# Attention on one Trainium2 core: score products as 32-row strips, one per head, with maxima and key mask added by accumulating products

## The reference

```python
N_HEAD = 16
qh = _split(q @ wq.T + bq)          # 8 x 16 x 256 x 8
kh = _split(k @ wk.T + bk)          # 8 x 16 x 512 x 8
vh = _split(v @ wv.T + bv)
scores = jnp.einsum('bhqd,bhkd->bhqk', qh, kh) / jnp.sqrt(jnp.float32(d_head))
# layer 2 only, one mask for all batches:
scores = jnp.where(mask == 0, jnp.float32(-1000000000.0), scores)
# layer 2, self-attention inside the feed-forward part: causal mask
# layer 3 only, one mask of keys per batch:
energy = jnp.where(mask == 0, jnp.float32(-1e+20), energy)
attn = jax.nn.softmax(scores, axis=-1)
out = jnp.einsum('bhqk,bhkd->bhqd', attn, vh)
return out.reshape(b, s, 128) @ wo.T + bo
```

## Time and profile before

| | us |
|---|---|
| median of 3 runs | 2374.96 |
| the 3 runs | 2376.47, 2366.19, 2374.96 |
| span of the profiled execution | 2364.8 |
| PE busy in it | 2118.7 (90%) |
| ACT busy | 1289.5 (55%) |
| DVE busy | 1247.3 (53%) |
| POOL busy | 499.4 (21%) |

### The profile page before, as it was taken

How to read it: one execution, slowest core, us unless ns; L and a number is a source line. 1 busy time by engine, 2 the same in 40 slices (tenths; PEclk the granted TensorE clock), 3 DMA queues, 4 the chain that set the end, 5 groups by cost and what they waited for, 6 DMA issues and landing times. The chain is left out here.

```text
span 2364.8 us, 46942 instructions
## 1 busy us (share of the span) xinstructions
PE 2118.7 (90%) x14264; PEld 1391.1 (59%) x14264; DVE 1247.3 (53%) x3806; ACT 1289.5 (55%) x2226; POOL 499.4 (21%) x1107
## 2 busy tenths in 40 slices
PE   2999975699997999979999978887997999989998
PEld 1555543355555889844554545555885555548887
DVE  5667646566662222256666544444564667642343
ACT  0777752377774444346666644444331787864443
POOL 4221210111211222121111111222232222212221
PEclk9999987699998999979999978788997899999999
DMA  3322310622310000052213011110003423300000
GB/s 81 90 80 54 94 29 0 169 71 64 89 40 10 1 0 0 1 143 67 69 45 85 28 41 42 54 54 10 0 0 101 119 72 76 89 1 1 4 4 10
DMA packets 101314, 117.53 MB, mean 50 GB/s; under 512 B 12710, under 2 KB 68412, under 8 KB 101180
## 3 DMA queue, kind: packets, MB, share of 16 engines
q1 hardware_dynamic: 101180, 115.94, 18.5%
HBM read 70.82 MB, written 45.09 MB: 49 GB/s over the span
## 5 line engine op out<-in xcount | busy, mean ns | idle before, releaser
L929 PE MATMUL ps_s<-kst,qz 96*128 96x512 f32 (+2 forms) x1280 | 601.2, 485 | 60.6 <-DMA qz<-q_parts 40.4
L758 ACT ACTIVATE prob<-ps_t 128x512 f32<-128x512 f32 (+1 forms) x896 | 492.3, 581 | 265.7 <-PE ps_t L941 109.9
L941 PE MATMUL ps_t<-qz,kst 128*128 128x512 f32 (+1 forms) x1152 | 464.5, 407 | 0.5 <-ACT prob L758 0.2
L1313 DVE CUSTOM_DVE_ANT_0 junk<-ps_s,mask_q 128x512 bf16<-128x512 f32 x512 | 342.1, 688 | 167.1 <-PE ps_s L929 160.4
L1304 DVE TENSOR_REDUCE mx<-ps_s 128x1 f32<-128x512 f32 x512 | 334.5, 684 | 138.5 <-PE ps_s L929 137.3
L929 PEld LDWEIGHTS ps_s<-kst,qz 96*128 96x128 f32 x1280 | 256.4, 205 | 237.1 <-DVE mx L1313 59.9
L961 PE MATMUL ps_av<-prob,vaug 128*32 128x256 f32 (+1 forms) x4608 | 363.5, 390 | 3.4 <-ACT avs L794 3.1
L1160 PEld LDWEIGHTS ps_s<-w_ffn,prob 128*128 128x128 f32 x2688 | 315.4, 192 | 8.7
L1160 PE MATMUL ps_s<-w_ffn,prob 128*128 128x128 f32 x2688 | 319.2, 276 | 0.0
L798 ACT ACTIVATE qz<-ps_m 32x1024 fp32r<-32x1024 bf16 x160 | 162.7, 1017 | 152.6 <-PE ps_m L971 149.0
L941 PEld LDWEIGHTS ps_t<-qz,kst 128*128 128x128 f32 x1152 | 225.0, 197 | 33.7 <-issue 9.8
(11 more groups left out here) (200 smaller groups left out, 2403.3 us busy)
## 6 DMA issues: line engine op xcount, KB each, us to landing
kst<-k_parts SPq DMA_DIRECT2D x32, 768.0 KB, 6.1
k_parts<-k_hi SPq DMA_DIRECT2D x64, 256.0 KB, 2.9
qz<-q_parts SPq DMA_DIRECT2D x160, 96.0 KB
q_parts<-q_hi SPq DMA_DIRECT2D x80, 128.0 KB, 2.4
ctxT<-in_ctxT SPq DMA_DIRECT2D x32, 256.0 KB, 4.7
k_parts<-k_lo SPq DMA_DIRECT2D x32, 256.0 KB, 2.9
q_parts<-q_lo SPq DMA_DIRECT2D x40, 128.0 KB, 2.4
w_ffn<-in_F_w SPq DMA_DIRECT2D x18, 256.0 KB, 3.9
```

The costliest lines, as they stand in the source:

```text
L758: nc.scalar.activation(dst, src, ACT.Exp, bias=bias).then_inc(sig["exp_done"], 1)
L929: pe.matmul(ps_s[TURN[i]][:, 0:nk], qz[p][0:96, g, j, q * 128:(q + 1) * 128], kst[p][0:96, g, 0:nk], start=True, stop=True).then_inc(sig[" ...
L941: mm = pe.matmul(dst, kst[p][:, g, kt * 128:(kt + 1) * 128], qz[p][:, g, 2 * half:2 * half + 2, q0:], start=True, stop=mask in (None, "keys"))
L1313: dve.tensor_tensor_reduce(junk[:, TURN[i], 0:nk], src, m, 1.0, -3.0e38, ALU.add, ALU.max, mx[:, buf, i:i + 1])\
```

## The change

- **Strips.** Each head of a group gets 32 partitions of its own: 24 rows of parts, and 8 rows that are ones in `kst` and zeros in q's stack, `qst`. The DRAM scratch has 32 rows per head; the 8 rows are filled once, by four DMAs from `q_lo` and `k_lo`, which POOL fills first. The memsets of `qz` and `kst` go, in the setup and at the start of A2 and A3.
- **s** (L952) becomes a row tile of 32 rows x 128 columns with 512 keys. The order of the eight is now heads 0, 1, 2, 3 for the first 128 queries, then for the others (`HEAD_S`).
- **MT** (L1003, L1005) is now one product that copies `qst` of the group into `ps_m` (by `ident_r`) and two bf16 products that add the transposed maxima in the eight rows of each head. ACT copies the sum into `qmx` (128 x 256, before 32 x 1024). POOL no longer negates, DVE's reduction does.
- **T** (L971) of a unit is one head and two key tiles, two products of 256 queries each on the head's strip, into one bank. The heads run in the order 2, 3, 0, 1 (`HEAD_T`), so a unit's s and T lie on different strips.
- **Key mask (A3).** After each s and each T comes a bf16 product with one row on the same strip and into the same bank (L955, L974), which adds the mask's row. POOL prepares one bf16 row per batch (`mrow`); DVE's maximum is the plain one, ACT's exponential has no bias.
- **Full mask (A2)** and **causal mask (AS)** (L977, L981) stay one product on 128 rows, after the two T of the unit. In AS a unit has 256 + 128 columns, four units a group, two at k = 0 and two at k = 3.
- **Splits.** But in AS, ACT reads a projection once (`kf`, `qf`), and POOL makes `k_hi` and `q_hi` from it and then the low part. SP's saves wait for POOL's copy.
- **Loads.** K's and q's stacks are loaded group by group, eight DMAs per batch on a semaphore per group, after both saves; s of a group waits for its own two.
- `prob` is now ordered by head, v (L995) reads it so; its products are the same.

```diff
+HEAD_S = [0, 1, 2, 3, 0, 1, 2, 3]
+HEAD_T = [2, 3, 0, 1, 2, 3, 0, 1]
...
-        qz = [sb(f"qz{p}", [128, NG, HG, S], F32R) for p in range(2)]
+        qst = [sb(f"qst{p}", [128, NG, S], F32R) for p in range(2)]
+        qmx = sb("qmx", [128, 2, S], F32R)
...
-            def load_k(ph, bt):
+            def load_strips(ph, bt):
+
                 p, nk = bt.parity, ATT[ph]["nk"]
                 sp.wait_ge(k_saved[p], saved(ph, bt))
-                rows = scratch["k"][p].rearrange("(g r) w -> r g w", g=NG)[:, :, 0:nk]
-                sp.dma_start(kst[p][0:HG * ROWS, :, 0:nk].bitcast(F32), rows).then_inc(k_stacked[p], 16)
...
                 sp.wait_ge(q_saved[p], saved(ph, bt))
-                for j in range(HG):
-                    rows = scratch["q"][p].rearrange("(g j r) w -> j r g w", g=NG, j=HG)[j]
-                    sp.dma_start(qz[p][ROWS * j:ROWS * (j + 1), :, j, :].bitcast(F32), rows).then_inc(q_stacked[p], 16)
+                for g in range(NG):
+                    sp.dma_start(kst[p][:, g, 0:nk].bitcast(F32), scratch["k"][p][128 * g:128 * (g + 1), 0:nk]).then_inc(stacked[p][g], 16)
+                    sp.dma_start(qst[p][:, g, :].bitcast(F32), scratch["q"][p][128 * g:128 * (g + 1), :]).then_inc(stacked[p][g], 16)
...
+                if ph != "AS":
+                    apart(pool)
+                    pool.tensor_copy(k_hi[:, 0:nk], kf[:, 0:nk]).then_inc(sig["k_hi_done"], 1)
+                pool.wait_ge(sig["k_hi_done"], cnt.at("k_hi_done", ph, bt))
+                pool.tensor_tensor(k_lo[:, 0:nk], kf[:, 0:nk], k_hi[:, 0:nk].bitcast(F32), ALU.subtract).then_inc(sig["k_lo_done"], 1)
...
-                pe.matmul(ps_s[TURN[i]][:, 0:nk], qz[p][0:96, g, j, q * 128:(q + 1) * 128], kst[p][0:96, g, 0:nk],
-                          start=True, stop=True).then_inc(sig["s_ready"], 1)
...
+                mm = pe.matmul(dst, qst[p][strip, g, q * 128:(q + 1) * 128], kst[p][strip, g, 0:nk],
+                               start=True, stop=ATT[ph]["mask"] != "keys")
+                if ATT[ph]["mask"] == "keys":
+                    mm = pe.matmul(dst, ones_b[STRIP * j:STRIP * j + 1, 0:128], mrow[STRIP * j:STRIP * j + 1, p, :], start=False, stop=True)
+                mm.then_inc(sig["s_ready"], 1)
...
-                mm = pe.matmul(dst, kst[p][:, g, kt * 128:(kt + 1) * 128], qz[p][:, g, 2 * half:2 * half + 2, q0:],
-                               start=True, stop=mask in (None, "keys"))
+                bank = ps_t[TURN[turn]]
+                for c in range(2):
+                    kt = 2 * kp + c
+                    dst = bank[:, S * c:S * (c + 1) - seen(ph, kt)]
+                    mm = pe.matmul(dst, kst[p][strip, g, kt * 128:(kt + 1) * 128], qmx[strip, g % 2, seen(ph, kt):],
+                                   start=c == 0 or mask in (None, "keys"), stop=mask is None)
+                    if mask == "keys":
+                        mm = pe.matmul(dst, mrow[STRIP * j:STRIP * j + 1, p, kt * 128:(kt + 1) * 128], ones_b[STRIP * j:STRIP * j + 1, :],
+                                       start=False, stop=True)
...
-                for j in range(HG):
-                    for q in range(QT):
-                        mm = pe.transpose(ps_mb[96:128, S * j + 128 * q:S * j + 128 * (q + 1)],
-                                          mpart[:, g % 2, q, 32 * j:32 * j + 32], ident_b[:, :])
+                pe.matmul(ps_m[:, 0:S], ident_r[:, :], qst[bt.parity][:, g, :], start=True, stop=False)
+                for q in range(QT):
+                    mm = pe.matmul(ps_m[:, 128 * q:128 * (q + 1)], mpart[:, g % 2, q, :], ident_b[:, :], start=False, stop=q == QT - 1)
```

More of the change, by code:

```diff
@@ L41 @@
 HG = 4
-ROWS = 3 * DH
+STRIP = 32
+PARTS = 3
 NG = H // HG
@@ L361, in seen, with pairs, unit, unit_at @@
             return 128 * kt if ph == "AS" else 0
-        def turn_of(ph, g, kt, half):
-            return (2 * (ATT[ph]["nk"] // 128 * g + kt) + half) % 8
+        def pairs(ph):
+            return ATT[ph]["nk"] // (2 * 128)
+        def unit(ph, g, n):
+            return HG * pairs(ph) * g + n
+        def unit_at(ph, k, half):
+            if pairs(ph) == 2:
+                return 2 * k + half
+            return {0: 0, 3: 2}[k] + half if k in (0, 3) else None
+        def chance(ph, g, n):
+            return prob[:, g % 2, HEAD_T[n], :], 2 * (n // HG)
         def slots(ph):
@@ L426, in _ @@
             load_attention("A0", loaded_first)
+            sp.wait_ge(setup_pool, 3)
+            for p in range(2):
+                for n, fill, w in (("q", q_lo, S), ("k", k_lo, SK)):
+                    rest = scratch[n][p].rearrange("(h b c) w -> b h c w", h=H, b=STRIP // DH)[PARTS]
+                    sp.dma_start(rest, fill[:, 0:w].bitcast(F32)).then_inc(strips_filled, 16)
             def load_rest():
@@ L748, in _, with exponentials @@
         def _(act):
-            def exponentials(ph, bt, g, kt, half):
-                p, nkt, q0 = bt.parity, ATT[ph]["nk"] // 128, seen(ph, kt)
-                bias = mcol[:, p, kt:kt + 1] if ATT[ph]["mask"] == "keys" else 0.0
-                wait(act, "st_ready", cnt.at("st_ready", ph, bt, 2 * (nkt * g + kt) + half))
-                if half == 0:
-                    wait(act, "av_ready", cnt.at("av_ready", ph, bt, nkt * g + kt) - 2 * nkt)
-                dst = prob[:, g % 2, kt, 2 * S * half:2 * S * (half + 1)].rearrange("p (j s) -> p j s", j=2)[:, :, q0:]
-                src = ps_t[TURN[turn_of(ph, g, kt, half)]][:, 0:2 * (S - q0)].rearrange("p (j s) -> p j s", j=2)
-                nc.scalar.activation(dst, src, ACT.Exp, bias=bias).then_inc(sig["exp_done"], 1)
+            def exponentials(ph, bt, g, n):
+                nkt = ATT[ph]["nk"] // 128
+                wait(act, "st_ready", cnt.at("st_ready", ph, bt, unit(ph, g, n)))
+                if n % HG == 0:
+                    wait(act, "av_ready", cnt.at("av_ready", ph, bt, nkt * g + 2 * (n // HG) + 1) - 2 * nkt)
+                row, kt = chance(ph, g, n)
+                w = 384 if ph == "AS" else 2 * S
+                nc.scalar.activation(row[:, S * kt:S * kt + w], ps_t[TURN[unit(ph, g, n) % 8]][:, 0:w], ACT.Exp).then_inc(sig["exp_done"], 1)
             def misc(what, ph, bt):
@@ L920, in scores @@
             def scores(ph, bt, g, i):
-                p, nk, j, q = bt.parity, ATT[ph]["nk"], i // 2, i % 2
-                if g == 0 and i == 0:
-                    pe.wait_ge(q_stacked[p], stacked(ph, bt, HG))
-                    pe.wait_ge(k_stacked[p], stacked(ph, bt, 1))
+                p, nk, j, q = bt.parity, ATT[ph]["nk"], HEAD_S[i], i // HG
+                strip = slice(STRIP * j, STRIP * (j + 1))
+                if i == 0:
+                    pe.wait_ge(stacked[p][g], loads_until(ph, bt))
+                    if ATT[ph]["mask"] == "keys" and g == 0:
+                        wait(pe, "mask_conv", cnt.at("mask_conv", ph, bt))
                 if ph == "AS":
@@ new lines, in scores, with scores_T @@
+                mm = pe.matmul(dst, qst[p][strip, g, q * 128:(q + 1) * 128], kst[p][strip, g, 0:nk],
[3 more added lines that the diff above has]
+                mm.then_inc(sig["s_ready"], 1)
+            def scores_T(ph, bt, g, n):
+                p, mask = bt.parity, ATT[ph]["mask"]
+                turn, j, kp = unit(ph, g, n) % 8, HEAD_T[n], n // HG
+                strip = slice(STRIP * j, STRIP * (j + 1))
+                if n == 0:
+                    wait(pe, "mt_read", cnt.at("mt_read", ph, bt, g))
+                wait(pe, "exp_done", cnt.at("exp_done", ph, bt, unit(ph, g, n)) - BACK[turn])
+                bank = ps_t[TURN[turn]]
[7 more added lines that the diff above has]
+                                       start=False, stop=True)
@@ L957, in values @@
                         wait(pe, "v_read", cnt.at("v_read", ph, bt))
[L958 removed]
+                wait(pe, "exp_done", cnt.at("exp_done", ph, bt, unit(ph, g, HG * (kt // 2) + HG - 1)))
                 buf = g % 2
```

153 lines of the change are left out of this document (69 added, 84 removed).

## The result

The changed kernel takes 2468.3 us (median of 4 runs, 2460.68 to 2516.44) against 2372.03 for the kernel before (4 runs), a ratio of 1.038, 95% interval 1.0337 to 1.0423: **slower by 96 us**, where -0.8% was forecast. The ratio leaves out the run of 2516.44, in which the clock was lower than in the other three. The profiled execution spans 2458.5 us, 93.7 more than before.

A forecast was written before the change was run, and what follows sets the result against it. PE sets the pace, DVE is the next wall. A0 and A1 -96, A3 +66, A2 +8, AS +15, starts -13 give -20: span 2345, plus 10 for the median, 2355 us; own range 2315 to 2395, with rivals 2310 to 2545.

The forecast's parts named there:

- Strips side by side: In A0 and A1, s and T on different strips overlap: minus 0.53 us per cycle, 2.12 per group.
- Rivals (1): Strips overlap in columns but their weight loads queue, 0.107 us each: 2448 us, slower; chance 0.14.
- (2): Strips don't overlap at all and a cycle gets 0.045 us longer: 2638 us; chance 0.09.
- Helpers and XT: Per batch, helper products cost 2.0 us in changes of shape; single ACT reads and time around XT give -0.85.
- The 0.2 per change of shape: Wherever tile shape changes between PE products, 0.09 us plus the open weight load is lost, 0.2 us.
- A3: The one-row key mask can't run beside the product it is added to: plus 0.45 us per cycle, +66 us.
- rival (4): A3's masks overlap after all, so A3 gains like A1, -48 instead of +66: 2241 us; chance 0.06.
- A2: The 128-row mask product sits between strips, 0.44 us each; the cycle wins nothing, helpers cost: +8 us.
- AS: Causal mask between short strips and helpers cost, less waiting for K's stack wins: +15 us, range -10 to +60.
- Starts: At stage starts, first scores wait for one group's load, not the whole stack, and A0 loses memsets: -13 us.
- rival (3): Strips use a quarter of the array, so A0 to A3 might fall to AS's granted clock, 0.81: 2546 us; chance 0.13.
- its last sign: The forecast is wrong altogether if A3 is not the stage that loses.

The follow-up runs named there:

- Run 4: Changed kernel with T's heads in the order 0, 1, 2, 3, so a unit's s and T share one strip: 3084.05 us, 1.298.
- run 8: Changed kernel with ACT making k_hi and q_hi in all stages again, POOL only the low parts: 2428.16 us.
- Run 1: Kernel before, with s and T reading only 32 rows of their stacks: 3315.75 us, 1.396 times before.
- runs 2: Kernel before, with five added VectorE reductions in the last group of every batch so that PE waits: 2488.29 us, 1.046.
- Run 9: Changed kernel with A3's mask in a spare strip row and fill products in PE's waits in A0 and A2: 2280.93 us, 0.962 of before.

## Why the prediction was wrong

- **What bounds it**: right in the main. PE set the pace, but for the last group of a batch, at DVE's 5.7 us (6.3 forecast), and A0's batch ends, where PE waited 1.4 us for DVE; A0's batches took 29.4 us at the full clock for that.
- **Strips side by side**, -0.53 a cycle: right in kind, too small in size. A cycle that nothing held up won 0.70 (1.71 to 1.01). A batch won 7.0 us (35.2 to 28.2), 29.2 was forecast, and not 16 x 0.70 = 11.2: the other 4.2 went to helpers and to turns with DVE, which no run takes apart. Run 4 shows it is the strip that matters. Rivals (1) and (2) fell, for the weight loads of different strips start within 0.01 us of each other too.
- **Helpers and XT**: the single read gave 0.5 and not 0.85 (run 8). The 0.2 per change of shape has no run of its own.
- **A3**, "so it can't run beside it": wrong. A mask waits for its own product, not for the other strips, and they all overlap. Mis-sized by 43.5 - 32.2 = 11.3 us a batch; rival (4), called unlikely, had the mechanism, if not at no cost.
- **A2**, 0.44 per mask: 0.36, so 40.6 a batch where 43 was forecast.
- **AS**, +15: measured +50, at the lower level throughout.
- **Starts**, -13: -15 with the F stages, but by luck. A0's first s came 9.2 us sooner (2 forecast) and the waits for the first strips fell by 3.1 to 3.3 us (3.8 forecast). In exchange PE now waited 9.2, 4.2 and 4.6 us for the second batch's context in A1, A2 and A3, before 2.5 or less. The forecast had no such term.
- **The step that failed** is the one that isn't in the sum: that the granted share stays where it was. It was rival (3), at 0.13, with the price 2546 at AS's share; measured were shares of 0.51 to 0.90 and 2468. I set against it that "v and the helpers, full-width, fill over half of the time". Run 1 has the same v and helpers and half the clock. What spoke for it, a wait of PE for DVE, was right as the start of A0's falls (runs 2 and 9), but A3's longest came without one. The forecast's own sign for (3), a share under 0.95, came true in A0, A1 and A3; by its last sign the forecast was wrong altogether, since A2 lost most and A3's loss was the clock's.

The loss adds up. From their batches at the full clock A0 and A1 would have won 16 x 7.0 = 112 us, A2 8 x 1.5 = 12 and A3 8 x 3.0 = 24; with the -15 beside the stages that is -163. AS lost 50. The profiled span grew by 93.7, so some 207 us went to A0 to A3 (41, 18, 82 and 66), to the lower clock and a smaller part to the waits above: A0's batch ends (1.4 us in six batches) and the second batches' context. Run 9 gives the check: with the clock held in A0 and A2 and the mask's row moved, the total is 187 us lower.

The range held the time, the sign was that of the rival. That it held is in part luck: the 2546 of rival (3) had A3's masks in it, 8 x 11.3 = 90 us too many, and left A2's and AS's losses out. The Trainium skill ("TensorE: Matmul & The Clock Gate", Part 1) ties the clock to how busy the engine was; the runs differ from that, with PE busy 99.5% at a share of 0.50 in run 1.

What stays open: how much of the array must be in use (no run measures it), whether rows or changes of shape weigh more in A2, why fills at the starts left A3 at the lower level, and how to bring AS back.
